# A GRU step on TensorE: the n gate's matrix and the state as three exact bf16 parts, and r, z, n made apart by halves

## The reference

```python
def cell(h, x):
    gi = x @ W_ih + b_ih
    gh = h @ W_hh + b_hh
    i_r, i_z, i_n = jnp.split(gi, 3, axis=-1)
    h_r, h_z, h_n = jnp.split(gh, 3, axis=-1)
    r = jax.nn.sigmoid(i_r + h_r)
    z = jax.nn.sigmoid(i_z + h_z)
    n = jnp.tanh(i_n + r * h_n)
    h_new = (1.0 - z) * n + z * h
    return (h_new, h_new)
...
x = x + _L0_cond_ref(x, ...)                     # attention
x = x + _L1_cond_ref(cond_2048, x, ...)          # the scan of cell over 512 steps
x = x + _L2_cond_ref(x, ...)                     # depthwise causal conv, 4 taps
x = x + _L3_cond_ref(x, ..., L3_cond_b)          # the same, with a bias
```

## Time and profile before

| | us |
|---|---|
| median of 3 runs | 2115.24 |
| lowest and highest | 2114.27, 2116.45 |
| span of the profiled execution | 2113.7 |
| recurrence, from its first matmul (572.4) to its last step (2105.6) | 1533 |

### The profile page before, as it was taken

One profiled execution on the slowest core, in us unless ns is written; L12 is line 12 of the kernel. 1 busy time (PEld: TensorE's weight loads), 2 busy tenths in 40 slices (PEclk: granted clock), 3 DMA queues, 4 the chain that ended last, 5 costly groups with the idle time before them and its releaser, 6 DMA issues.

```text
span 2113.7 us, 181503 instructions
## 1 busy us (share of the span) xinstructions
PE 2071.9 (98%) x77848; PEld 1578.9 (75%) x77848; DVE 1354.9 (64%) x6162; ACT 1239.1 (59%) x5995; POOL 638.0 (30%) x1015
## 2 busy tenths in 40 slices
PE   8999999999999999999999999999999999999998
PEld 2222222222499999999999999999999999998887
DVE  4344445444367777777777777777777777776676
ACT  3445544443266666666666666666666666666665
POOL 0355547444112222222222222222222222222222
PEclk9999999999999999999999999999999999999999
DMA  6000000011222222221222222222121212210001
GB/s 259 1 1 1 1 1 1 1 60 31 49 54 53 52 55 52 52 55 49 69 59 55 52 53 53 56 58 66 50 58 50 58 48 60 67 30 11 5 8 20
DMA packets 218082, 96.04 MB, mean 45 GB/s; under 512 B 170216, under 2 KB 213480, under 8 KB 217320
## 3 DMA queue, kind: packets, MB, share of 16 engines
q1 hardware_dynamic: 217032, 92.00, 16.8%
q10 hardware_dynamic: 928, 2.65, 0.3%
HBM read 26.30 MB, written 12.58 MB: 18 GB/s over the span
## 4 chain that ended last, share of the span: by engine, by line
PE 70%; DVE 2%; issue 0%; DMA 0%; ACT 0%; SPq 0%; DVEq 0%
PE ps L1241 64%; PE ps L1274 4%; PE ps L1282 2%; DVE arena L1069 1%; DVE arena L1087 0%; DMA arena<-arena 0%; DVE arena L965 0%; DVE arena L1075 0%; DVE arena L1082 0%; DVE arena L968 0%; ACT arena L1210 0%; SPq L994 0%; DVE arena L1158 0%; DVE seq L1163 0%; DVE seq L1100 0%
## 5 line engine op out<-in xcount | busy, mean ns | idle before, releaser
L1241 PE MATMUL ps<-whh,arena 128*4 128x128 f32 (+1 forms) x65568 | 1451.4, 246 | 13.8 <-issue 1.6
L1241 PEld LDWEIGHTS ps<-whh,arena 128*4 128x4 f32 x65568 | 1293.6, 87 | 112.2 <-DVE arena L1087 25.8
L1069 DVE STREAM_TRANSPOSE arena<-ps 128x64 f32<-128x64 f32 x2048 | 446.4, 284 | 256.1 <-PE ps L1241 237.0
L1199 ACT ACTIVATE arena<-arena 128x8 f32<-128x8 f32 x1024 | 216.1, 211 | 543.4 <-DVE arena L1069 480.1
L455 DVE TENSOR_REDUCE top<-ps 128x2 f32<-128x1024 f32 x128 | 150.8, 1220 | 244.0 <-PE ps L722 244.0
L1174 ACT ACTIVATE ps<-arena 128x128 f32<-128x128 f32 x1026 | 288.9, 282 | 0.5 <-PEq L212 0.4
L1087 DVE TENSOR_TENSOR_SCAN arena<-arena 128x24 f32<-128x24 f32 x1024 | 192.1, 188 | 145.1 <-ACT arena L1210 145.1
L1075 DVE STREAM_TRANSPOSE arena<-ps 128x64 f32<-128x64 f32 x1024 | 257.5, 251 | 9.0 <-PE ps L1241 3.3
L361 ACT ACTIVATE arena<-ps 128x1024 f32<-128x1024 f32 x128 | 124.1, 1021 | 212.7 <-PE ps L798 212.6
L610 PE MATMUL ps<-arena 128*32 128x512 f32 x2048 | 242.7, 595 | 2.7 <-ACT arena L383 2.7
L965 POOL TENSOR_TENSOR arena<-tap,arena 128x128 f32<-128x128 f32 x252 | 102.0, 415 | 430.0 <-DVE seq L1100 430.0
(11 more groups left out here) (99 smaller groups left out, 1268.0 us busy)
## 6 DMA issues: line engine op xcount, KB each, us to landing
arena<-arena SPq DMA_DIRECT2D x216, 114.0 KB, 2.2
arena<-arena SPq DMA_DIRECT2D x112, 128.0 KB
arena<-seq SPq DMA_DIRECT2D x224, 55.0 KB
arena<-gi_d SPq DMA_DIRECT2D x248, 32.0 KB
gi_d<-arena SPq DMA_DIRECT2D x96, 57.0 KB
out<-seq SPq DMA_DIRECT2D x14, 256.0 KB
seq<-in_x SPq DMA_DIRECT2D x3, 1024.0 KB, 15.6
whh<-in_w_hh SPq DMA_DIRECT2D x1, 3072.0 KB, 21.1
```

Of the source, the lines that this page charges most:

```text
L1069: e.transpose(trn[:, h, q].rearrange("p (i c s) -> p c i s", c=2, s=2)[:, :, :, 0], bank[RN[h]][:, 64 * q:64 * q + 64].rearrange("p (c i) ...
L1199: e.activation(r_d0[:, h].rearrange("p (i s) -> p i s", s=2)[:, :, 1], trn[:, h, 0, 0:2 * NH].rearrange("p (i s) -> p i s", s=2)[:, :, 0], ...
L1241: last = e.matmul(bank[dst[h]][32 * G:32 * G + B, 0:n], hv, wv[:, k, gates, G, 64 * h:64 * h + 64], start=False, stop=k2 == 1 and k == C - ...
```

## The change

- The columns of W_hh for the n gate are held as three bf16 parts whose sum is the f32 number (`wn3`). POOL makes them in the attention stage, one chunk of 512 at a time (`split_weights`), after n = 2, 3, 6 and 7.
- The state is held as three parts too. The first part is the upper two bytes of the f32 number, read in place as bf16; `second` takes it from the number and leaves the rest, whose upper two bytes are the second part; `third` does it once more. Both are new DVE instructions, two for each half.
- The n product takes 16 fixed columns (4 batches by 3 parts and one that is zero) and three streams of the moving operand, in bf16: nine products. The parts come out in separate PSUM rows, and `scan_n`, now over groups of five instead of two (40 numbers instead of 16), adds them up before it multiplies by r.
- r, z and n have a bank for each half, six in all, each 64 columns wide. `begin` makes r and z of half 0, r of half 1 and n of half 0 from half 0 of the state. `end` finishes r, z and n of half 0, then makes n of half 1 from half 1 of the state, r of half 1, n of half 1 from half 0, and z of half 1.
- A chunk body has two steps instead of four, and half the columns of r and z (57 instead of 114); there are 224 bodies. DVE's operations for chunks (`gate_ops`) stand between `second(0)` and `third(0)` instead of behind the step.
- The bias of n is held once (`bhn`) and copied into PSUM by ACT, instead of standing in the ring; the ring has 4096 numbers a partition to clear instead of 6144.

```diff
-        whh = sb("whh", [P, C, 3 * D])
+        whh = sb("whh", [P, C, 2 * D])
+        whn = sb("whn", [P, D])
+        wn3 = sb("wn3", [P, C, PARTS, D], BF16)
...
+
+                    wait(s_whn, 16 * k + 16)
+                    for i in range(PARTS):
+                        if i:
+                            wait(g_whn, SPLIT_OPS * k + 2 * i - 1)
+                            e.tensor_tensor(whn[:], whn[:], wn3[:, k, i - 1], ALU.subtract).then_inc(g_whn, 1)
+                            wait(g_whn, SPLIT_OPS * k + 2 * i)
+                        e.tensor_copy(wn3[:, k, i], whn[:]).then_inc(g_whn, 1)
...
+                e.memset(r_d0.rearrange("p h (i s) -> p (h i) s", s=NS5)[:, :, 1:HW], 1.0).then_inc(c, 1)
...
-        AW, NW = 114, 55
+        AW, NW = 57, 55
...
-        BODIES = 2 * len(N_BLOCKS)
+        BODIES = C * len(N_BLOCKS)
+        AK = (slice(0, C - 1), slice(C - 1, C))
...
+                    def turn_n(h):
+                        e.wait_ge(st["s_n"], half[h])
+                        e.transpose(trn[:, h].rearrange("p (b c s) -> p c b s", c=2, s=NS5)[:, :, :, 0:HW],
+                                    bank[N[h]][:, 0:64].rearrange("p (c b s) -> p c b s", c=2, s=HW)).then_inc(st["s_tn"], 1)
...
                     def scan_n(h):
-                        e.wait_ge(st["s_tr"], n_at[h])
-                        e.wait_ge(st["s_sig"], half[h])
-                        e.tensor_tensor_scan(pre[:, h], r_d0[:, h], trn[:, h, 1, 0:2 * NH], 0.0,
+                        for name in (("s_tn", "s_sig"), ("s_sig", "s_tn"))[h]:
...
+                    def second(h):
+                        e.wait_ge(st["s_h"], h_half[h])
+                        rest(e, 1 - u, h, 0).then_inc(st["s_top"], 1)
+
+                    def third(h):
+                        e.wait_ge(st["s_top"], half[h])
+                        rest(e, 1 - u, h, 1).then_inc(st["s_p"], 1)
+
+                    turn_r(0)
                     turn_z(0)
+                    turn_n(0)
                     scan_n(0)
-                    turn_rn(1)
+                    turn_r(1)
+                    turn_n(1)
                     scan_h(0)
                     turn_z(1)
                     scan_n(1)
+                    second(0)
+                    gate_op()
+                    third(0)
                     scan_h(1)
-                    e.wait_ge(st["s_h"], h4)
-                    x_now = seq[:, :, bass.ds(now, 1)].rearrange("p (h c b) t -> p h c (b t)", h=2, c=2)
-                    e.tensor_tensor(x_now, x_now,
-                                    hb[:, 1 - u, :, 0:HS].rearrange("p h (b c s) -> p h c b s", c=2, s=3)[:, :, :, :, 2],
-                                    ALU.add).then_inc(st["s_x3"], 1)
+                    second(1)
+                    third(1)
+                    x_now = seq[:, :, bass.ds(now, 1)].rearrange("p (h i) t -> p h (i t)", h=2)
+                    e.tensor_tensor(x_now, x_now, hf[:, 1 - u, :, 2 * HW:2 * HW + HI * (NH - 1) + 1:HI], ALU.add
+                                    ).then_inc(st["s_x3"], 1)
...
+                def gate_ops(t):
+
+                    q, v = divmod(t, 2)
+                    if v == 1 and q < BODIES:
+                        take_rz(q)
+                    if v == 0 and q % C == 0 and 0 < q <= BODIES:
+                        take_n(q // C - 1)
+                        if q < BODIES:
+                            seed_n(q // C)
...
                         reset(0)
-                        e.wait_ge(st["s_tr"], turned[1])
-                        seed_rn(0, s)
+                        seed_r(0, s)
+                        e.wait_ge(st["s_tz"], half[0])
+                        seed_z(0, s)
                         update(0)
                         new(0)
+                        e.wait_ge(st["s_tn"], half[0])
+                        seed_n(0)
                         reset(1)
-                        e.wait_ge(st["s_tr"], turned[4])
-                        seed_rn(1, s)
+                        seed_r(1, s)
                         update(1)
                         new(1)
-                        seed_z(0, s)
+                        e.wait_ge(st["s_tn"], half[1])
+                        seed_n(1)
+                        bring(following)
+                        e.wait_ge(st["s_tz"], half[1])
                         seed_z(1, s)
-                        bring(following)
...
+                def products_n(u, h, k2, stop):
+
+                    for k in (2 * k2, 2 * k2 + 1):
+                        hv = parts_of(u, k)
+                        for s in range(PARTS):
+                            for G in range(NG):
+                                last = e.matmul(bank[N[h]][32 * G:32 * G + HW * B, 0:64], hv, wp[:, k, s, G, 64 * h:64 * h + 64],
+                                                start=False, stop=stop and k % 2 == 1 and s == PARTS - 1, skip_group_check=True)
+                    return last
...
                     e.wait_ge(st["s_h"], half[0])
-                    e.wait_ge(st["s_seed_rn"], half[0])
-                    products(u, RN, rn, 0, 0)
-                    e.wait_ge(st["s_seed_rn"], half[1])
-                    products(u, RN, rn, 1, 0)
+                    e.wait_ge(st["s_seed_r"], half[0])
+                    products(u, R, 0, 0, 0)
+                    e.wait_ge(st["s_seed_z"], half[0])
+                    products(u, Z, 1, 0, 0)
+                    e.wait_ge(st["s_seed_r"], half[1])
+                    products(u, R, 0, 1, 0)
+                    e.wait_ge(st["s_p"], half[0])
+                    e.wait_ge(st["s_seed_n"], half[0])
+                    products_n(u, 0, 0, False)
 
                 def end(t, u):
                     half = (count(2 * t + 1), count(2 * t + 2))
                     e.wait_ge(st["s_h"], half[1])
-                    products(u, RN, rn, 0, 1).then_inc(st["s_rn"], 1)
-                    e.wait_ge(st["s_seed_z"], half[0])
-                    products(u, RZ, z, 0, 0)
-                    products(u, RZ, z, 0, 1).then_inc(st["s_z"], 1)
-                    products(u, RN, rn, 1, 1).then_inc(st["s_rn"], 1)
+                    products(u, R, 0, 0, 1).then_inc(st["s_r"], 1)
+                    products(u, Z, 1, 0, 1).then_inc(st["s_z"], 1)
+                    e.wait_ge(st["s_p"], half[1])
+                    products_n(u, 0, 1, True).then_inc(st["s_n"], 1)
+                    e.wait_ge(st["s_seed_n"], half[1])
+                    products_n(u, 1, 1, False)
+                    products(u, R, 0, 1, 1).then_inc(st["s_r"], 1)
+                    products_n(u, 1, 0, True).then_inc(st["s_n"], 1)
                     e.wait_ge(st["s_seed_z"], half[1])
-                    products(u, RZ, z, 1, 0)
-                    products(u, RZ, z, 1, 1).then_inc(st["s_z"], 1)
+                    products(u, Z, 1, 1, 0)
+                    products(u, Z, 1, 1, 1).then_inc(st["s_z"], 1)
```

232 lines of the change are left out of this document (123 added, 109 removed).

## The result

The changed kernel takes 2267.1 us (median of 4 runs, 2262.9 to 2269.1) against 2115.5: ratio 1.071, 95% interval 1.070 to 1.073. The forecast was 2080, its range ended at 2170. Both the sign and the size were wrong. The profiled execution's span is 2260.7 us, 147.0 over that of before.

The account below looks back on a forecast made before the run. Two limits meeting at 2.97 us a step, PE's own work and a chain of waits through DVE, were to fall to 2.91 with chunks and 2.85 without: 35.3 us off, 2080 us, range 2040 to 2170.

Parts of the forecast that it names:

- the sum: Whole kernel: 26.9 us from 448 chunk steps, 7.7 from 64 without, 0.7 in front; 35.3 off the span.
- each cost at nothing: Beside the recurrence: POOL's weight chunks (8.3 us, up to 11) and SP's DMAs (3.2 of 5.8 us) counted as hidden.
- Rival B: DVE's part of the chain is dearer, deciding from a scan of some 0.27: +22 us, 2137; chance 0.22.
- The chain of half 0: From begin through PE, n transpose, scan, tanh and state scan back to PE: 2.82 us a step.
- the n transpose: DVE's transpose in the chain, behind n of half 0: 0.28 us, with 0.25 as the other end.
- The copies' stall: Chunk copies out of PSUM ahead of third(0): stall 0.10 us every second step, 0.27 with two copies every eighth.
- Pitches: PE's start-to-start times: 57 ns a narrow f32 quad, 30 ns a short bf16 quad.
- rival C: Short bf16 streams miss their 30 ns pitch: 2195 us at 40 ns, +300 us at 57; chance 0.15.
- the 40 scan: DVE's scan of 40 numbers for n: taken as 0.245 us, expected at 0.23 to 0.26 in the profile.
- PE waiting for L209: In begin, PE was to wait for L209 by 0.03 to 0.27 us.
- Rival A: PE becomes the bound at 2.83 us, scan at 0.19 and no stalls: 2040 us; chance 0.11.
- Rival D: PE's changed order makes the chunks' loads by SP late: 2190 us; chance 0.04.

Follow-up runs that it names:

- the cut in the kernel before: Kernel before the change, TensorE's loops cut behind z of half 1 or the chunk instead of behind begin's eight wide quads: 2144.7 us, ratio 1.0136.
- the empty loop: Changed kernel plus a one-pass empty loop behind begin's n products, in the chunk-stage step that had no branch there: 2301.8 us.
- early: Changed kernel with GpSimd's operations of positions 1 to 7 of a batch started about 0.4 us earlier: 2246.9 us.
- small: Changed kernel with GpSimd's convolution operations in the recurrent loop on 8 columns instead of 128, all waits kept: 2242.6 us.
- one load: Changed kernel with GpSimd early, loops cut behind z or chunk, chunk pieces and copies moved; a body's two r/z operand loads issued as one DMA: 2202.5 us.
- late copies: Changed kernel with GpSimd early, and VectorE's chunk copies behind third of half 0, the n seed copy behind the last operation: 2245.5 us.
- five kernels that no theory ordered: Changed kernel with GpSimd early, loops, chunk pieces and copies moved; two r/z loads, one, no n, no r/z, none: 2230.3, 2202.5, 2233.9, 2192.8, 2206.2 us.
- n in f32: Changed kernel with GpSimd early, and the n gate's products as 4 narrow f32 quads in place of 6 bf16 ones: 2249.4 us.
- cut at n: Changed kernel with GpSimd early, and TensorE's loops cut in front of begin's n products instead of behind them: 2250.4 us.

## Why the prediction was wrong

The step that failed is the sum: it has PE's work as matmuls only ("PE's work goes from 2.68 to 2.54 us"), and no term for TensorE's sequencer. The runs showed 0.41 us without a matmul's start at the branch in every second step, some 104 us, and 25 us of stops. The earlier trace rows show a step of the kernel before with a branch in it and no gap. I read that as "the loop costs nothing"; it was hidden by the wide quads that the change removes. I listed what hides each cost at nothing, and not what hid the loop.

From the forecast's steps to the measured ones it is 448 x (3.27 - 2.91) + 64 x (3.16 - 2.85) = 182 us; entering the second loop (the first step in it takes 6.98 us) and a later start give some 7. The span is 182 over the forecast's and not 189, since the forecast took 2.97 us for a step of the kernel before, which by the measure used here has 2.98. The 182 us of the steps:

- Branch: 0.41 us in 224 even steps with a chunk, 0.37 in 32 without (where 0.045 of the gap would have been a wait): 104. Shown by the records, by the cut in the kernel before and by the empty loop. No run is without it in the steps with chunks, so there the 0.41 is read from the records.
- Scans held by GpSimd: 31 by the records. The early and small runs gave back 20 and 25, or 23 and 29 less their stops. Rival B asked for a slower scan and set the point from its length (0.27); it is 0.24, and became 0.5 through what runs beside it.
- The chain of half 0: 2.91 without any trouble, not 2.85, 512 x 0.06 = 31. PE's segments from `begin` to n of half 0 in `end` take 1.52, forecast 1.50 and a stall of 0.025. From there to the n transpose it is 0.30, not 0.23: 0.05 of it is DVE's three transposes, which follow each other at 0.225 us while PE's pieces for them come 0.22 and 0.17 apart. The state scan takes 0.21, not 0.17. The transpose (0.25 for 0.28) and the waits around the scan (0.035 for 0.06) give 0.05 back.
- Stops in mid-stream, in the steps with chunks: 25, added up from the records.
- The copies' stall came out smaller (0.37 us in one step of eight, nothing in the others: 0.046 a step against 0.065), which takes 8 off. The five make 183.

Point by point. Pitches: right. 16 narrow f32 starts take 0.223 us (56 ns a quad), 24 bf16 starts 0.174 (29 a quad). Where two n streams follow each other the second takes 0.243 (40 a quad): rival C in a small way, in the one place where 48 short matmuls come in a row. The starts are 7.3 ns apart, so the floor of about 25 ns in the Trainium skill ("TensorE: Matmul & The Clock Gate", "Wait — 56ns, not 53.3ns?") can hold for a column group at most, as the forecast had it. The n transpose (0.25) and the 40 scan (0.24): right. PE waiting for L209: not at all in a plain step, and 0.37 with two copies, against 0.03 and 0.27. What it waits for by 0.045 in a plain step is the state scan of half 1, in `end`:

```profile
2198.36 0.21 DVE L1140 TENSOR_TENSOR_SCAN arena<-arena 128x24 f32<-128x24 f32 x1
```

The scan ends 0.84 us behind `begin`, whose first load stands in the first timeline above at 2197.73, and the first load of `end`, at 2198.62, follows 0.05 later. The forecast had it "ready at about 0.7", though by its own terms `third(0)` ends at 0.65 and the scan stands behind it: its length was left out.

The work ahead of the recurrence was 0.7 us less in the forecast. Its first matmul does start earlier, by 0.3 us (572.07 against 572.35). But the first step is done at 579.1 us, before 576.2, and within it TensorE stands for 2.46 us in front of an r or z product, labelled "issue". Rival A never came up. Rival D, at 4 in 100, said that SP's loads would be late. They aren't: chunk matmuls wait for a DMA once in the whole run, by 0.5 us. But the loads' issues go with stops of TensorE, which "one load" shows to be worth 28 us in a kernel that has little else left. The place was right, the mechanism not.

The second half of the change is worth next to nothing here: with f32 n products in the bf16 ones' place, the time is 2249.4 against 2246.9. The shorter pieces do save time: less their stops the two runs are 2237.5 and 2215.5, 22 us apart. But the bf16 kernel has 31 us of stops and the f32 one 15, and the f32 one has a smaller gap at the branch (0.35 from start to start, against 0.41).

What stays open is the mechanism of the stops. They depend on the matmul stream (half as much with f32 n), on SP's r/z loads (54 us with two, 26 with one, 21 with none), and on a store split in two (158 us against 31, which is 127 of its 134 us in the profiled runs). They need no r/z or n loads at all (35 us without). Whether it is the issue, the descriptors, the arrival of the data or the supply of TensorE's own instructions wasn't told apart.

## What to carry to other kernels

Before splitting wide matmuls into short ones, look where the engine's loop branches and how much queued work lies ahead of it: here a taken branch wants some 0.45 us of it, and more if waits follow. Put the branch where the engine waits anyway, and check each stage, since work that fills the wait uncovers the branch. When a fix gives back less than its cost, add up the idle time labelled "issue" inside the streams in both profiles before dropping the theory: it ate the gain of the late copies, and less the stops five kernels that no theory ordered came out alike. And when an operation on VectorE gets a new place in time, look at what GpSimd does at that moment.

## What the runs showed of the hardware

- The lead of TensorE's sequencer over the matmuls follows the length of what is queued: 0.43 us behind wide f32 quads (before), 0.14 (n in f32) and 0.20 (cut at n) behind narrow ones, 0.05 to 0.07 behind bf16 streams of 64 columns (after, early). From the first record of the branch to the next weight load it takes 0.47 us, and 0.56 to 0.59 where a wait with a record of its own stands between.
- VectorE's scan of 40 numbers, with two SBUF inputs, never ends less than 92 ns after a GpSimd tensor_tensor that ran when it started. In 1658 of 1659 such scans, in 16 traces, its length is 0.24 us or, if that is longer, what it takes to end 0.096 us after GpSimd's operation, to within 4 ns. A transpose out of PSUM at the same moments takes 0.26 us at most, as always. The Trainium skill calls the port pair of the two an exclusive lock that whoever starts first has for the whole instruction ("SBUF — State Buffer", "SBUF: two separate sides"). The traces agree, for the scan that comes second: GpSimd's operation takes 0.42 to 0.46 us, so one that starts over 0.31 us into it is 0.24 us long only because its end would lie behind GpSimd's anyway.
- A TensorE loop of 1952 loads and matmuls is fetched again in each pass (137 packets of 16 KB in 15 passes) and takes more than twice the time, at a mean clock of 0.84; in one of 1792 every second pass takes 30 us and the others 13; one of 1152 isn't fetched again.
- TensorE's stream stops in the middle with no semaphore: by 15 to 158 us in the steps with chunks, and not once in 56 steps without, in all 16 kernels that were counted.
